# Two node stages of a graph network kernel: work on whole groups of four tiles, or tile by tile

## The chip, the core and the metric

The kernel runs on one core of a Trainium2 chip. The metric is the device time of one execution in microseconds, the median of several runs. The profile is of one execution, taken by the hardware profiler.

## The reference, cut to what matters

Four graph layers follow each other. In each, a node stage makes dense products from normalized node features, and an edge stage gathers and sums over 50000 edges. The node features are `x`, 50000 rows of 256 float32.

```python
def _layernorm(x, axis=-1, eps=1e-05):
    m = jnp.mean(x, axis=axis, keepdims=True)
    v = jnp.var(x, axis=axis, keepdims=True)
    return (x - m) / jnp.sqrt(v + eps)
...
h = jnp.maximum(_layernorm(x), 0.0)
x = x + _L0_gnn_ref(h, ...)
h = jnp.maximum(_layernorm(x), 0.0)
x = x + _L1_gnn_ref(h, ...)      # ends: agg + h @ w_own + bias
h = jnp.maximum(_layernorm(x), 0.0)
x = x + _L2_gnn_ref(h, ...)      # needs h @ W_s.T, h @ W_t.T; ends: agg @ W_fc.T + b_fc
h = jnp.maximum(_layernorm(x), 0.0)
x = x + _L3_gnn_ref(h, ...)      # needs h @ W_forward.T, h @ W_reverse.T
```

The bias of the second layer (`own_bias`) is added to its output only when the third node stage reads it, and the third layer's `b_fc` is added there too, ahead of its time, to the copy of x that the third edge stage will add to (`both_bias` is the sum of the two).

## The kernel before

`node_pass(layer)` is the node stage, called four times with `layer` 0 to 3. The third and the fourth node stage are layers 2 and 3. The rows are cut into tiles of 128 rows (one to a partition) by 256 columns. Four tiles (`G` = 4) make a group, and there are 98 groups. Every buffer with the suffix of a side exists four times (`S` = 4): group c uses side c mod 4, so a side is free again when its use by group c-4 is over.

Each engine runs its own program over the groups through `pipeline`, which takes pairs of a lag and a function. At step c it calls each function on group c minus its lag, in the order of the list. With `by_tile` it calls them all for tile 0, then all for tile 1, and so on. Most steps stand in a hardware loop of four steps, one for each side. Engines meet in semaphores that count up: `then_inc` when an instruction is done, `wait_ge` ahead of the next one.

In layers 2 and 3 the work of a group is this:

- SP loads `x` of the group (L1667). In layer 2 it waits for `bias_in` of the group four before, in layer 3 for `normed` of it. At the end it stores the results: in layer 2 `from_src` and `to_dst` (the two products, L1703), `own` (the tile `biased`, L1699) and `turned` (the rectified and transposed tiles `kept_t`, L1705), 512 KB each; in layer 3 only `h`, 272 KB (L1703). A store waits for `out_made`, ACT's copies of all four tiles. In SP's list, the load of group c comes before the store of group c-6. Every store counts up `t_put` of its side when it has landed.
- DVE, step c, list `[(norm_lag, normalize), (0, average)]` with `norm_lag` = 2: first `normalize` of group c-2, four instructions `tensor_scalar` for `xn` (L1784), the last of which counts up `normed`. Then `average` of group c. In layer 2 `average` begins with `join`: it waits for `x`, for `normed` and for `t_put` of group c-4, and then adds `own_bias` to the whole group for `xc` (L1759) and `both_bias` for `biased` (L1760), each one instruction over 128 x 1024 elements. Then come four `bn_stats` (L1770), four `bn_aggr` (L1774) and one addition for `var` (L1777). Layer 3 has no `join` work: its statistics read `x` itself.
- POOL takes `var` to the power -0.5 (L1890). In layer 2 it also copies keys and issues four indirect stores a group (L1903).
- PE, `work` of group q: for each tile g it first turns the next tile (two transposes of `xn`, L1955; behind tile 3 that is tile 0 of the next group), then does the products of tile g (four matmuls, L1977). `turn` waits for `normed`, the whole group, in layers 2 and 3.
- ACT rectifies each turned tile (L2016) and copies the products of each tile to `out` (L2032 in layer 2, L2035 in layer 3).

In layers 0 and 1 DVE already works by tile, with `normalize_tile` and `average_tile`, and PE is told of each normalized tile by `normed_tile`. In layer 0 DVE's order for each tile is normalizing (L1848), bias on the product (L1861), statistics (L1790).

Of the kernel before, what the change touches and what calls it, by code (L numbers as in the profile page):

```python
# [5 lines left out]
ALU = mybir.AluOpType  # L6
# [6 lines left out]
P = 128  # L13
# [3 lines left out]
D = 256  # L17
# [817 lines left out]
G = 4  # L835
# [59 lines left out]
def pipeline(engine, groups, stages, apart=0, by_tile=False):  # L895

    deepest = max(lag for lag, _ in stages)  # L900
    looped = (groups - apart) // S
    peel = min(looped, -(-(deepest + S) // S))

    def step(i, c):
        live = []
        for lag, stage in stages:
            side = (c - lag) % S
            uses = i + (c - lag - side) // S
            H = uses * S + side
            if isinstance(H, int) and not 0 <= H < groups:  # L910
                continue
            live.append((stage, Group(H, side, uses, groups)))
        for g in range(G if by_tile else 1):
            for stage, q in live:
                stage(q, g) if by_tile else stage(q)

    for s in range(S * peel):
        step(s // S, s % S)
    if looped > peel:
        with engine.Fori(peel, looped) as i:  # L920
            for c in range(S):
                step(i, c)
    for s in range(S * looped, groups + deepest):
        step(s // S, s % S)
# [663 lines left out]
def node_pass(nc, k, layer, x_in, mixed_in=None, tables=()):  # L1588
# [5 lines left out]
    groups = k.NT // G  # L1594
    n_put = len(tables)
# [6 lines left out]
    x = both("x", [P, G, D])  # L1602
    if layer == 1:
        xc, mixed = both("xc", [P, G, D]), both("mixed", [P, G, D])
        small = [[ph.sb(f"small{h}_{n}", [P, G]) for n in range(12)] for h in range(S)]
# [7 lines left out]
    xn = both("xn", [P, G, D])  # L1613
# [36 lines left out]
    with nc.Block() as block:  # L1650
# [63 lines left out]
        def _(dve):  # L1714
# [30 lines left out]
                steps(nc.vector.scalar_tensor_tensor(s[11][:], s[2][:], 1.0, s[7][:], ALU.add, ALU.mult))  # L1745
                steps.end()

            def across(bias):

                return bias[:].rearrange("p (o f) -> p o f", o=1).to_broadcast([P, G, D])  # L1750

            def join(q):

                dve.wait_ge(x_got[q.h], 16 * (q.i + 1))
                if layer == 2:
                    if not q.new:
                        dve.wait_ge(normed, q.last)
                        dve.wait_ge(t_put[q.h], 16 * n_put * q.i)
                    nc.vector.tensor_tensor(xc[q.h][:], x[q.h][:], across(k.own_bias), ALU.add).then_inc(joined, 1)  # L1759
                    nc.vector.tensor_tensor(biased[q.h][:], x[q.h][:], across(k.both_bias), ALU.add).then_inc(bias_in, 1)  # L1760
                    dve.wait_ge(joined, q.H + 1)

            def average(q):

                join(q)
                if not q.new:
                    dve.wait_ge(normed, q.last)
                steps = Steps(dve, averaging, q.H, 2)
                for g in range(G):
                    ins = nc.vector.bn_stats(stats[q.h][:, g, :], source[q.h][:, g, :])  # L1770
                steps(ins)
                dve.sem_inc(stats_in, 1)
                for g in range(G):
                    ins = nc.vector.bn_aggr(moments[q.h][:, g, :], stats[q.h][:, g, :])  # L1774
                steps(ins)
                steps.end()
                nc.vector.tensor_scalar(var[q.h][:], moments[q.h][:, :, 1], 1e-5, None, ALU.add).then_inc(var_made, 1)  # L1777

            def normalize(q):
                dve.wait_ge(std_made, q.H + 1)  # L1780
                if not q.new:
                    dve.wait_ge(turned, G * q.last)
                for g in range(G):
                    ins = nc.vector.tensor_scalar(xn[q.h][:, g, :], source[q.h][:, g, :], moments[q.h][:, g, 0:1],  # L1784
                                                  inv_std[q.h][:, g:g + 1], ALU.subtract, ALU.mult)
                ins.then_inc(normed, 1)

            def tile_stats(q, g):

                return nc.vector.bn_stats(stats[q.h][:, g, :], source[q.h][:, g, :])  # L1790
# [1 line left out]
            def average_tile(q, g):  # L1792

                if g == 0:
                    dve.wait_ge(x_got[q.h], 16 * (q.i + 1) + (16 if layer == 1 and q.final and x_in.shape[0] % P else 0))
                    if not q.new:
                        dve.wait_ge(normed, q.last)
                        if layer == 1:
                            dve.wait_ge(raw_made, G * q.last)
                    if layer == 1:  # L1800
                        ball(q)
                if layer == 1:
                    ins = nc.vector.scalar_tensor_tensor(xc[q.h][:, g, :], mixed[q.h][:, g, :], small[q.h][11][:, g:g + 1],
                                                         x[q.h][:, g, :], ALU.mult, ALU.add)
                    if g < G - 1:
                        ins.then_inc(join_tile, 1)
                    else:
                        ins.then_inc(joined, 1)
                    if g:
                        dve.wait_ge(join_tile, (G - 1) * q.H + g)  # L1810
                        dve.sem_inc(mean_in, 1)
                        tile_stats(q, g - 1)
                    if g < G - 1:
                        return
                    dve.wait_ge(joined, q.H + 1)
                    dve.sem_inc(mean_in, 1)
                ins = tile_stats(q, g)
                if g < G - 1:
                    return
                steps = Steps(dve, averaging, q.H, 2)  # L1820
                steps(ins)
                dve.sem_inc(stats_in, 1)
                for n in range(G):
                    ins = nc.vector.bn_aggr(moments[q.h][:, n, :], stats[q.h][:, n, :])
                steps(ins)
                steps.end()
                nc.vector.tensor_scalar(var[q.h][:], moments[q.h][:, :, 1], 1e-5, None, ALU.add).then_inc(var_made, 1)  # L1827
# [46 lines left out]
            if layer == 1:  # L1874
                pipeline(dve, groups, [(2, clamp_tile), (norm_lag, normalize_tile), (after_lag, own_tile),
                                       (join_lag, average_tile)], by_tile=True)
            elif layer == 0:
                pipeline(dve, groups, [(norm_lag, normalize_tile), (after_lag, bias_tile), (0, average_tile),
                                       (after_lag + 2, pair_tile)], by_tile=True)
            else:  # L1880
                pipeline(dve, groups, [(norm_lag, normalize), (0, average)])

        @block.gpsimd
        def _(pool):
# [58 lines left out]
        @block.tensor  # L1943
        def _(pe):
            def turn(q, g):

                t = G * q.H + g
                if layer <= 1 and g < G - 1:
                    pe.wait_ge(normed_tile, (G - 1) * q.H + g + 1)
                else:  # L1950
                    pe.wait_ge(normed, q.H + 1)
                if not (q.first and g < 2):
                    pe.wait_ge(rectified, t - 1)
                for c in range(2):
                    ins = nc.tensor.transpose(p_turn[g % 2][:, c * P:(c + 1) * P], xn[q.h][:, g, c * P:(c + 1) * P],  # L1955
                                              k.ident[:])
                ins.then_inc(turned, 1)

            def work(q):

                if q.first:
                    turn(q, 0)
                for g in range(G):
                    t = G * q.H + g
                    if g + 1 < G:
                        turn(q, g + 1)
                    elif not q.final:
                        turn(q.next(), 0)
                    pe.wait_ge(rectified, t + 1)
                    if not (q.first and g < banks):  # L1970
                        if layer <= 1:
                            pe.wait_ge(raw_made, t - banks + 1)
                        if layer >= 1:
                            pe.wait_ge(out_made, t - banks + 1)
                    for w, (n, matrix) in enumerate(k.products[layer]):
                        for c in range(2):
                            ins = nc.tensor.matmul(p_out[w][g % banks][:, 0:n], turned_rows(q.h, g)[:, c * P:(c + 1) * P], matrix[:, c, :],  # L1977
                                                   start=c == 0, stop=c == 1)
                    ins.then_inc(product, 1)
            pipeline(pe, groups, [(work_lag, work)], apart=2)  # L1980
# [785 lines left out]
```

## Time and profile before

| | |
|---|---|
| median of 3 runs | 8104.73 us |
| the runs | 8104.73, 8105.07, 8094.45 us |
| profiled execution | 8095.47 us |
| its span | 8093.8 us |
| instructions | 150708 |
| PE busy | 5806.9 us (72%) |
| DVE busy | 5259.3 us (65%) |
| ACT busy | 3347.9 us (41%) |
| POOL busy | 4865.0 us (60%) |
| third node stage in the span | about 3840 to 4665 us |
| fourth node stage in the span | about 6649 to 7005 us |

The shares are means over stages with different limits; what a stage is bound by is read from its own stretch. All times in the rows are microseconds from the start of the span unless a column says ns. PE is matrix work, PEld its loading of weights, DVE the vector engine, ACT the scalar engine, POOL the general engine, SP the engine that issues most transfers (its queue is SPq).

### The profile page before, as it was taken

The numbers are of one execution on the slowest core, as the hardware profiler recorded it, in microseconds if no ns is written. First come the engines' busy times: TensorE is split into PE (matmuls) and PEld (weight loads), VectorE is DVE, ScalarE is ACT, GpSimd is POOL, SyncE is SP. The second block draws the span as 40 slices with busy tenths as digits, with TensorE's granted clock in tenths as the row PEclk, the third lists the DMA queues.
The fourth block names the chain that finished last, engine by engine and source line by source line (L and its number), as shares of the span: only waits on it lengthen the run. The fifth ranks groups of instructions, "written<-read, shape, count | busy, mean of one in ns | idle before, by whom it ended". The sixth has DMA issues, their size and how long they took to land. (4 is left out here: it accounts for less than half of the span.)

```text
span 8093.8 us, 150708 instructions
## 1 busy us (share of the span) xinstructions
PE 5806.9 (72%) x21870; PEld 3548.2 (44%) x21871; DVE 5259.3 (65%) x17471; ACT 3347.9 (41%) x10587; POOL 4865.0 (60%) x6155
## 2 busy tenths in 40 slices
PE   4997899326769999677899967777666779500477
PEld 3773344115544444455444434444224558500365
DVE  4999888324559998355666657666773559633755
ACT  1992255203555554255344433333112567400166
POOL 1556777747652222775777767777467753477443
PEclk7996799668899999899999988988897999855799
DMA  1662000026877776687888866666106878522167
GB/s 60 211 211 57 1 1 1 1 65 220 287 248 243 249 246 231 210 291 272 293 316 317 310 203 202 204 203 204 38 16 215 297 270 229 155 55 55 51 225 238
DMA packets 803185, 1457.11 MB, mean 180 GB/s; under 512 B 137216, under 2 KB 543597, under 8 KB 803030
## 3 DMA queue, kind: packets, MB, share of 16 engines
q1 hardware_dynamic: 462070, 752.88, 28.2%
q10 hardware_dynamic: 188000, 410.91, 14.7%
q0 software_dynamic: 152960, 291.84, 12.9%
q14 instruction: 129, 1.06, 0.0%
q8 instruction: 26, 0.43, 0.0%
HBM read 809.53 MB, written 645.70 MB: 180 GB/s over the span
## 5 line engine op out<-in xcount | busy, mean ns | idle before, releaser
L1280 PE MATMUL merge_banks<-merge_rows,merge_mask 128*128 x6264 | 1607.3, 413 | 648.1 <-SPq L1249 436.0
L1280 PEld LDWEIGHTS merge_banks<-merge_rows,merge_mask 128*128 128x128 f32 x6264 | 1243.5, 205 | 1011.9 <-issue 831.3
L1421 POOL DMA_INDIRECT merge_rows<-h,merge_take_i x1224 | 1173.7, 959 | 472.6 <-issue 316.8
L1262 DVE TENSOR_SCALAR merge_mask<-ramp,dst_at,soft_at_step 128x128 f32<-128x128 f32 x2349 | 851.8, 369 | 912.4 <-PE merge_banks L1280 778.5
L1977 PE MATMUL node_p_out<-w,node_h_t 128*128 128x259 f32 (+2 forms) x4704 | 1433.9, 427 | 14.3 <-ACT node_h_t L2016 12.9
L1344 ACT COPY merge_total<-merge_banks 128x256 f32<-128x256 f32 x1568 | 577.2, 369 | 1076.3 <-PE merge_banks L1280 931.8
L1890 POOL TENSOR_TENSOR node_inv_std<-node_var,node_minus_half 128x4 f32<-128x4 f32 x392 | 453.6, 1157 | 863.1 <-DVE node_var L1827 570.6
L1977 PEld LDWEIGHTS node_p_out<-w,node_h_t 128*128 128x128 f32 x4704 | 745.0, 190 | 267.4 <-issue 212.5
L1955 PE MATMUL node_p_turn<-ident,node_xn 128*128 128x128 f32 x3136 | 619.6, 279 | 189.1 <-DVE node_xn L1784 91.2
L1977 PE MATMUL node_p_out<-w,node_kept_t 128*128 128x512 f32 x1568 | 741.0, 595 | 0.0
L1955 PEld LDWEIGHTS node_p_turn<-ident,node_xn 128*128 128x128 f32 x3136 | 404.1, 141 | 737.7 <-issue 450.7
L1331 ACT COPY merge_banks<-merge_held 128x256 f32<-128x256 f32 x1568 | 587.9, 376 | 258.6 <-issue 134.4
L2207 PE MATMUL score_table<-score_at_high,score_at_low 128*128 128x392 f32 x784 | 387.2, 578 | 287.3 <-DVE score_at_high L2163 278.6
L1903 POOL DMA_INDIRECT src_sorted<-node_key,node_key_at x392 | 420.3, 1072 | 180.1 <-issue 92.7
L2016 ACT ACTIVATE node_h_t<-node_p_turn 128x256 f32<-128x256 f32 x1176 | 448.9, 382 | 142.8 <-PE node_p_turn L1955 137.5
L587 POOL DMA_INDIRECT rank_src_of_src<-ends,rank_src_take_src x392 | 373.7, 953 | 130.8 <-issue 122.8
L593 POOL DMA_INDIRECT rank_src_of_dst<-ends,rank_src_take_dst x392 | 377.2, 962 | 112.0 <-issue 104.7
L2143 POOL DMA_INDIRECT score_b<-to_dst,score_take_b x392 | 372.0, 949 | 119.4 <-issue 119.4
L2141 POOL DMA_INDIRECT score_a<-from_src,score_take_a x392 | 378.8, 966 | 105.0 <-issue 90.3
L2215 PE MATMUL score_p_h<-w,score_h_t 128*128 128x256 f32 x1568 | 440.7, 407 | 0.0
L2326 POOL DMA_INDIRECT score_a<-h,score_take_a x392 | 374.4, 955 | 106.1 <-issue 62.0
L1260 DVE TENSOR_SCALAR merge_mask<-ramp,dst_at 128x128 f32<-128x128 f32 x783 | 292.5, 397 | 201.2 <-PE merge_banks L1280 145.8
(541 smaller groups left out, 10536.2 us busy)
## 6 DMA issues: line engine op xcount, KB each, us to landing
merge_held<-own ACTq DMA_DIRECT2D x196, 512.0 KB, 5.4
x<-merge_total ACTq DMA_DIRECT2D x196, 512.0 KB
node_x<-x SPq DMA_DIRECT2D x196, 512.0 KB, 6.0
node_x<-in_x SPq DMA_DIRECT2D x194, 512.0 KB
h<-node_rows_h SPq DMA_DIRECT2D x98, 512.0 KB, 4.2
merge_held<-h ACTq DMA_DIRECT2D x98, 512.0 KB
mix<-merge_total ACTq DMA_DIRECT2D x98, 512.0 KB
node_mixed<-mix SPq DMA_DIRECT2D x98, 512.0 KB, 3.6
```

The source lines that it names most:

```text
L1262: ins = nc.vector.tensor_scalar(mask[j][:], k.ramp[:, 0:P], columns(k.dst_at, s), columns(weight, s), ALU.is_equal, ALU.mult)
L1280: nc.tensor.matmul(banks[:, bass.ds(nc.s_assert_within(at[2 * j + 1], 0, (BANKS - 1) * 512, skip_runtime_bounds_check_because=small), D)], ...
L1331: nc.scalar.copy(bank(q, g), held[q.held][:, g, :]).then_inc(seeded, 1)
L1344: nc.scalar.copy(total[q.total][:, g, :], bank(q, g)).then_inc(kept, 1)
L1421: nc.gpsimd.indirect_dma_start(rows[:, (j + n) * D:(j + n + 1) * D], None, table, bass.IndirectOffsetOnAxis(take_i[:, j + n:j + n + 1], 0) ...
L1890: nc.gpsimd.tensor_tensor(inv_std[q.h][:], var[q.h][:], minus_half[:], ALU.pow).then_inc(std_made, 1)
L1903: nc.gpsimd.indirect_dma_start(k.src_sorted, bass.IndirectOffsetOnAxis(key_at[:, g:g + 1], 0), key[:, g:g + 1], None, bounds_check=k.NP - ...
L1955: ins = nc.tensor.transpose(p_turn[g % 2][:, c * P:(c + 1) * P], xn[q.h][:, g, c * P:(c + 1) * P], k.ident[:])
L1977: ins = nc.tensor.matmul(p_out[w][g % banks][:, 0:n], turned_rows(q.h, g)[:, c * P:(c + 1) * P], matrix[:, c, :], start=c == 0, stop=c == 1)
L2016: nc.scalar.activation(turned_rows(q.h, g), p_turn[g % 2][:, 0:D], ACT.Relu).then_inc(rectified, 1)
L2207: nc.tensor.matmul(p_table[:, 0:NT], at_low[j % HOT][:], at_high[j % HOT][:], start=first and j == 0, stop=False, skip_group_check=True).t ...
L2215: ins = nc.tensor.matmul(p_h[j % 2][:, 0:D], h_t[side][:, g, c * P:(c + 1) * P], k.w2[:, c, 2 * D:3 * D], start=c == 0, stop=c == 1)
```

## The change

Layers 2 and 3 now use the functions by tile. `join`, `average` and `normalize` (and `across`, which spreads a bias over four tiles) go away. `average_tile` gets layer 2's part: for each tile one addition of `own_bias` for `xc` and one of `both_bias` for `biased`, then the statistics of the tile before. `bias_in` is counted up with the fourth tile's addition. The waits for `normed` and `t_put` of the group four before stand ahead of tile 0's additions. In the list of DVE, `normalize_tile` of group c-2 and `average_tile` of group c are called in turn for each tile. PE's `turn` waits for `normed_tile` for tiles 0 to 2 and for `normed` for tile 3, in all layers.

```diff
-            def across(bias):
-                return bias[:].rearrange("p (o f) -> p o f", o=1).to_broadcast([P, G, D])
-            def join(q):
-                dve.wait_ge(x_got[q.h], 16 * (q.i + 1))
-                if layer == 2:
-                    if not q.new:
-                        dve.wait_ge(normed, q.last)
-                        dve.wait_ge(t_put[q.h], 16 * n_put * q.i)
-                    nc.vector.tensor_tensor(xc[q.h][:], x[q.h][:], across(k.own_bias), ALU.add).then_inc(joined, 1)
-                    nc.vector.tensor_tensor(biased[q.h][:], x[q.h][:], across(k.both_bias), ALU.add).then_inc(bias_in, 1)
-                    dve.wait_ge(joined, q.H + 1)
-            def average(q):
...
-            def normalize(q):
...
@@ average_tile
                         dve.wait_ge(normed, q.last)
                         if layer == 1:
                             dve.wait_ge(raw_made, G * q.last)
+                        elif layer == 2:
+                            dve.wait_ge(t_put[q.h], 16 * n_put * q.i)
                     if layer == 1:
                         ball(q)
-                if layer == 1:
-                    ins = nc.vector.scalar_tensor_tensor(xc[q.h][:, g, :], mixed[q.h][:, g, :], small[q.h][11][:, g:g + 1],
-                                                         x[q.h][:, g, :], ALU.mult, ALU.add)
+                if layer in (1, 2):
+                    if layer == 1:
+                        ins = nc.vector.scalar_tensor_tensor(xc[q.h][:, g, :], mixed[q.h][:, g, :], small[q.h][11][:, g:g + 1],
+                                                             x[q.h][:, g, :], ALU.mult, ALU.add)
+                    else:
+                        ins = nc.vector.tensor_tensor(xc[q.h][:, g, :], x[q.h][:, g, :], k.own_bias[:], ALU.add)
                     if g < G - 1:
                         ins.then_inc(join_tile, 1)
                     else:
                         ins.then_inc(joined, 1)
+                    if layer == 2:
+                        ins = nc.vector.tensor_tensor(biased[q.h][:, g, :], x[q.h][:, g, :], k.both_bias[:], ALU.add)
+                        if g == G - 1:
+                            ins.then_inc(bias_in, 1)
                     if g:
                         dve.wait_ge(join_tile, (G - 1) * q.H + g)
                         dve.sem_inc(mean_in, 1)
@@ the list of DVE
             else:
-                pipeline(dve, groups, [(norm_lag, normalize), (0, average)])
+                pipeline(dve, groups, [(norm_lag, normalize_tile), (0, average_tile)], by_tile=True)
@@ PE
             def turn(q, g):
                 t = G * q.H + g
-                if layer <= 1 and g < G - 1:
+                if g < G - 1:
                     pe.wait_ge(normed_tile, (G - 1) * q.H + g + 1)
                 else:
                     pe.wait_ge(normed, q.H + 1)
```

## Rows read from the trace of the kernel before

**Rows 1.** Two stretches: PE, PEld, DVE, ACT, POOL busy; clock, DMA share, GB/s.

```profile
3900.00:4600.00 700.00, 665.41 (x2018) 309.78 (x2017) 474.66 (x1260) 297.74 (x672) 531.48 (x595) 1.00 0.89 315
...
6680.00:6980.00 300.00, 283.01 (x2044) 243.13 (x2043) 274.42 (x1109) 216.58 (x681) 102.39 (x85) 1.00 0.82 228
```

**Rows 2.** Groups of instructions by line, 3900 to 4600: busy, mean ns, idle before and releaser.

```profile
L1955 PE MATMUL node_p_turn<-ident,node_xn 128*128 128x128 f32 x672 | 131.3, 277 | 34.6 <-DVE node_xn L1784 34.4
...
L1890 POOL TENSOR_TENSOR node_inv_std<-node_var,node_minus_half 128x4 f32<-128x4 f32 x85 | 107.1, 1260 | 11.8 <-DVE node_var L1777 10.8
L1759 DVE TENSOR_TENSOR node_xc<-node_x,own_bias 128x1024 f32<-128x1024 f32 x84 | 103.5, 1232 | 200.3 <-DMA turned<-node_kept_t 200.3
```

**Rows 3.** Timeline of DVE, third stage: start, us, instruction, idle before it and releaser.

```profile
3909.63 1.23 DVE L1759 TENSOR_TENSOR node_xc<-node_x,own_bias 128x1024 f32<-128x1024 f32 x1 [2.09 <-DMA turned<-node_kept_t]
...
4101.67 1.23 DVE L1759 TENSOR_TENSOR node_xc<-node_x,own_bias 128x1024 f32<-128x1024 f32 x1 [2.58 <-DMA turned<-node_kept_t]
...
4103.95 1.40 DVE L1770 BATCH_NORM_STATS2 node_stats<-node_xc 128x6 f32<-128x256 f32 x4
...
4106.52 1.38 DVE L1784 TENSOR_SCALAR node_xn<-node_xc,node_moments,node_inv_std 128x256 f32<-128x256 f32 x4 [0.41 <-issue]
4109.27 1.23 DVE L1759 TENSOR_TENSOR node_xc<-node_x,own_bias 128x1024 f32<-128x1024 f32 x1 [1.37 <-DMA turned<-node_kept_t]
...
4113.71 1.43 DVE L1784 TENSOR_SCALAR node_xn<-node_xc,node_moments,node_inv_std 128x256 f32<-128x256 f32 x4
4118.65 1.23 DVE L1759 TENSOR_TENSOR node_xc<-node_x,own_bias 128x1024 f32<-128x1024 f32 x1 [3.52 <-DMA turned<-node_kept_t]
...
4633.21 1.23 DVE L1759 TENSOR_TENSOR node_xc<-node_x,own_bias 128x1024 f32<-128x1024 f32 x1 [2.02 <-DMA turned<-node_kept_t]
```

**Rows 4.** Timeline of SP's issues, third stage.

```profile
3901.93 0.38 SPq L1703 DMA_DIRECT2D from_src<-node_out  x1
...
4111.07 0.38 SPq L1703 DMA_DIRECT2D from_src<-node_out  x1
...
4626.26 0.38 SPq L1703 DMA_DIRECT2D from_src<-node_out  x1
```

**Rows 5.** Timelines of PE and ACT, third stage.

```profile
4108.03 0.43 PE L1955 MATMUL node_p_turn<-ident,node_xn 128*128 128x128 f32 x2 [0.82 <-DVE node_xn L1784]
...
4110.05 0.38 PE L1955 MATMUL node_p_turn<-ident,node_xn 128*128 128x128 f32 x2
...
4110.25 0.58 ACT L2032 COPY node_out<-node_p_out 128x512 f32<-128x512 f32 x1 [1.36 <-PE node_p_out L1977]
...
4112.18 0.58 ACT L2032 COPY node_out<-node_p_out 128x512 f32<-128x512 f32 x1 [1.07 <-PE node_p_out L1977]
```

**Rows 6.** Timeline of DVE, fourth stage.

```profile
6656.59 1.41 DVE L1770 BATCH_NORM_STATS2 node_stats<-node_x 128x6 f32<-128x256 f32 x4 [3.50 <-DMA node_x<-x]
...
6800.74 1.38 DVE L1784 TENSOR_SCALAR node_xn<-node_x,node_moments,node_inv_std 128x256 f32<-128x256 f32 x4
...
6802.03 1.40 DVE L1770 BATCH_NORM_STATS2 node_stats<-node_x 128x6 f32<-128x256 f32 x4
...
6804.10 1.38 DVE L1784 TENSOR_SCALAR node_xn<-node_x,node_moments,node_inv_std 128x256 f32<-128x256 f32 x4
```

**Rows 7.** Timelines of PE and SP, fourth stage.

```profile
6802.25 0.43 PE L1955 MATMUL node_p_turn<-ident,node_xn 128*128 128x128 f32 x2
6802.30 0.34 SPq L1667 DMA_DIRECT2D node_x<-x  x1
```

**Rows 8.** Timeline of DVE, first node stage.

```profile
404.41 0.42 DVE L1861 TENSOR_TENSOR node_out<-node_p_out,bias 128x259 f32<-128x259 f32 x1
404.75 0.41 DVE L1790 BATCH_NORM_STATS2 node_stats<-node_x 128x6 f32<-128x256 f32 x1
405.08 0.39 DVE L1848 TENSOR_SCALAR node_xn<-node_x,node_moments,node_inv_std 128x256 f32<-128x256 f32 x1
```

**Rows 9.** Transfers issued 6680 to 6980: KB each, median us from issue to landing.

```profile
h<-node_out SPq DMA_DIRECT2D x85, 272.0 KB, 4.3
```

More of the change, by code:

```diff
@@ L1746, in ball @@
                 steps.end()
-            def across(bias):
-                return bias[:].rearrange("p (o f) -> p o f", o=1).to_broadcast([P, G, D])
-            def join(q):
-                dve.wait_ge(x_got[q.h], 16 * (q.i + 1))
-                if layer == 2:
-                    if not q.new:
-                        dve.wait_ge(normed, q.last)
-                        dve.wait_ge(t_put[q.h], 16 * n_put * q.i)
-                    nc.vector.tensor_tensor(xc[q.h][:], x[q.h][:], across(k.own_bias), ALU.add).then_inc(joined, 1)
-                    nc.vector.tensor_tensor(biased[q.h][:], x[q.h][:], across(k.both_bias), ALU.add).then_inc(bias_in, 1)
-                    dve.wait_ge(joined, q.H + 1)
-            def average(q):
[L1765 to L1777, printed above, removed]
-            def normalize(q):
[L1780 to L1786, printed above, removed]
             def tile_stats(q, g):
```

## The prediction

> **What bounds the kernel now.** The change touches only two of the kernel's stages, the node passes of the third and the fourth layer, so I read first the table by stage [rows 1]. Third stage (steady part, 700 us): PE busy 665, DVE 475, DMA share 0.89. Fourth (300 us): PE busy 283, DVE 274. PE looks like the bound in both, but the question in each is who makes it wait.
>
> Third stage, groups of instructions with the idle time before them [rows 2]. 84 groups of four tiles in 700 us: 8.33 us a group. PE waits 34.4 us for `xn`, which is DVE's normalizing; DVE itself waits 200.3 us, 2.4 us a group, before `xc`, and what ends that is the DMA of `turned`, the last of the four stores of the group that used the same side four groups earlier. POOL waits for DVE's variance only 10.8 us in 700. So DVE isn't short of time; it stands behind a landing. The timeline shows the circle. DVE starts `xc` at 4101.67 and ends the normalizing at 4107.90 [rows 3]; PE starts the turn at 4108.03, and the next turn at 4110.05; ACT's copy starts at 4110.25 and takes 0.58; SP issues the store of that group at 4111.07 [rows 4, 5]; it has landed when DVE starts `xc` again, 4118.65 [rows 3]. Sum of the steps: 6.23 + 0.13 + 2.22 (turn, four products, up to ACT's copy) + 0.58 + 0.24 + 7.58 = 16.98 us, for **two** groups. It is two because of places: DVE's `xc` of group c needs the store of c-4; behind it in program order stands the normalizing of c-1, whose tile 0 PE turns before the last tile of c-2, and that tile completes the store on which `xc` of c+2 waits. In the step of 4101.67 DVE came round its loop (4106.52 is 0.4 late); without that the `xc`-to-normalized time is 5.87 (4109.27 to 4113.71 + 1.43). Landing, from the first store's issue to `xc`, is 7.41 us in the mean of 88 pairs; 7.70 in the first of them (3901.93 to 3909.63), 6.95 in the last (4626.26 to 4633.21), 7.58 in the one above [rows 3, 4]. With 7.41 the circle is 16.45 without the turn of the loop and 16.81 with it; half of the mean of both is 8.31, against the 8.33 measured. So the circle through the landing is the bound, not PE, whose own pace is 1.94 a tile (ACT's copies 4110.25 and 4112.18 [rows 5]), 7.74 a group.
>
> Fourth stage. DVE's instructions stand back to back: normalizing 6800.74, statistics 6802.03, next normalizing 6804.10 [rows 6], 3.36 us a group, with some 0.15 between statistics and their aggregate and a gap at the turn of the loop, once in four groups. PE starts its first turn 0.13 after the fourth normalized tile ends (6802.25 against 6802.12) [rows 6, 7]. PE follows DVE there, and DVE waits for nobody: `turned` of four groups back is long there, and 274 us busy with those short gaps fill the 300. DVE's own instructions are the bound.
>
> **The change part by part.** *Fourth stage, order.* Four normalizings, four statistics, four aggregates, one variance: none added or removed. Alone they follow each other every 0.32 (1.38 for four) and 0.33 [rows 6]; interleaved, in the first stage, product-plus-bias, statistics and normalizing start 0.34 and 0.33 after each other [rows 8]. So DVE's 3.36 stays. PE is told of the first tile 1.0 us earlier, but four tiles still come every 3.36, and PE's four take 3.33 (283 us for 85 groups). Gain: only at the very end, the last group, about 1 us. The increments per tile cost nothing beside [rows 8], where they are already made. *What comes later:* `normed` is now told after seven instructions instead of four, at 2.38 instead of 1.38, and the load of `x` waits for it (SP issues at 6802.30 what was told at 6802.12 [rows 7]); the first statistics of the step come at 0.33 instead of 1.30. The load has 2 x 3.36 - 2.38 - 0.18 + 0.33 = 4.5 us instead of 6.5. How long such a load takes isn't shown inside the stage, since nobody waits for it. Bounds: 3.5 on free engines (the first load of the stage [rows 6]), and 4.3 plus some for one that meets a store (the median of the store of `h` [rows 9]). I take 3.5 to 4.3, hidden, cost 0, because the store goes out behind the load, and the one before it went 2.7 us earlier. At 5.0 it would cost (5.0 - 4.5)/2 x 96 = 24 us.
>
> *Third stage, size.* `xc` and `biased` for 1024 elements start every 1.14 ((4103.95 - 4101.67)/2) [rows 3]; an addition of one tile takes 0.34 [rows 8], eight of them 2.7 instead of 2.28: 0.4 us more on DVE in each group. The wait for the tile before is always over (one tile behind), so I set it at nothing; at 0.05 each it would be 0.2 a group, on the old circle only. In the old circle PE no longer waits for the fourth normalized tile but for tile 0, three normalizings less (0.97); but three normalizings of the group before now lie in the body ahead of it (0.97 more). Both cancel, the 0.4 stays, and the old circle would become 17.0 in the mean. That alone is slower than 16.63.
>
> *Third stage, order.* This is the main term. Before, all four tiles of group c-2 were normalized ahead of the wait for the landing of c-4. Now only tile 0 is; tiles 1 to 3 come behind that wait. Queued behind it on DVE: `xc` and `biased` of tile 0, then normalizing 1, done 2 x 0.335 + 0.40 = 1.07 after the landing; tile 2 comes 1.33 later, tile 3 again 1.33, faster than PE's 1.94. Who waits for it: PE's turn of tile 1, and behind that in its queue the product of tile 0 and everything after. New circle: 1.07 + 0.13 + four tiles of PE from the turn of tile 1 up to ACT's last copy (2.02 to the next turn, as 4108.03 to 4110.05, twice 1.94, then 2.13 to the copy, as 4110.05 to 4112.18 [rows 5]: 8.03) + 0.58 + 0.24 + 7.41 = **17.46 us** for the two groups from c-4 to c-2. Nothing of it depends on the loop's turn. Half is 8.73, above the other circle's 8.5; both parities of groups stand under it, while before only one at a time was late. Against 8.33: +0.40 in each of the 94 groups with a landing wait, +38 us. What hides a part: nothing, PE would now wait 1.0 a group.
>
> What could shift the 7.41: with a longer group the same 2.5 MB meet fewer others; the load of `x` waits for `biased` of all four tiles, told 4.5 after the landing instead of 2.3, and goes right behind the four stores as before. Ends from the rows: 6.95, (17.00/2 - 8.33) x 94 = +16 us; 7.70, (17.75/2 - 8.33) x 94 = +51 us. I take the mean of the 88.
>
> The Trainium skill (Perfetto Trace Analysis, Optimizing Scalar/DVE Operations) gives about 60 ns of access overhead for each DVE instruction on SBUF; six more would be an estimated 0.36 us a group where the rows give 0.40, and the sum stays.
>
> **The rivals.** *Faster:* DVE isn't saturated, and PE's 34.4 us of waiting in 700 go, because tile 0 is ahead of the landing wait and told early. That would be 40 us over the 815 us of the stage if PE's 7.74 became the pace, but POOL has only 10.8 us of waiting in 700 [rows 2], which leaves 13; I put it at 8075. It decides if the landing falls under 16.66 - 10.05 = 6.61 us, below each of the three shown. The page just named says that where DVE isn't saturated but makes bubbles on others, breaking up instructions may let work end sooner. Its condition holds here (DVE 475 of 700), its effect needs the broken-up work to lie ahead of the wait, and three of four tiles don't. 10%. *Same:* the landing shrinks to 6.9 or less as stores spread evenly, or PE's wait and the landing overlap better than in the circle: +0 to +16, 14%, about 8108. *Slower still:* as forecast, and the fourth stage's load comes late: DVE waits before its statistics; decides from a load of 4.5 us on, at 5.0 +24 on top, about 8160. The overlap of load and store speaks for it, the DMA share of 0.82 [rows 1] against. 14%.
>
> **How the numbers follow.** The profiled execution takes 8095.5 (span 8093.8). +38 in the third stage, -1 at the end: 8133 (8132.5). The runs' median is 8104.7, two of three near 8105 and one at 8094.5, so I set 4 on top of the profiled time's sum: **8137**. Forecast 62%. The range: from +16 on the profiled execution, less 4 for the lowest run, 8108, to +51 with the higher runs and a part of the last rival, 8168. A difference within 0.2%, 16 us, is about what measurement of this kernel can't tell from none. Faster 0.10, same 0.14, slower 0.76.
>
> **What would show it.** Third stage: 8.6 to 8.9 us a group; PE waits of about 1 us before a turn in nearly every group (before: about every second group), and the turn that waits is the second of a group, not the first; DVE idle before `xc` still ended by `turned`; `xc` a tile op of 0.4 us. Fourth stage: DVE step 3.36 still, PE's wait for `xn` spread thinner, no wait for `x`. Wrong: if landings are under 6.9 us, or if DVE waits for `x` in the fourth stage, or if the third stage's group takes under 8.3.

## The result and the profile after

The changed kernel takes 8175.95 us in the median (8165.82 to 8192.45), the kernel before 8099.59 us in the median of the runs beside it. The ratio is 1.0097, with a 95% interval from 1.0084 to 1.011: slower, by 76 us where 32 were forecast (8137 against 8104.7), and outside the range (8108 to 8168). The profiled execution took 8173.59 us, its span is 8171.9 us, 78 more than before.

The third node stage, from the first clearing of `x` to the first clearing of the stage behind it, took 844.4 us before (3840.07 to 4684.44) and takes 928.7 us now (3828.51 to 4757.21): +84.3. The fourth, up to POOL's first copy behind it, went from 360.3 to 362.3 us. So all of it is in the third.

The steady part of the third stage, as a stretch of 600 us. Columns as in [rows 1]: busy us (instructions) of PE, PEld, DVE, ACT, POOL, then TensorE's granted clock, DMA share, GB/s.

```profile
3950.00:4550.00 600.00, 533.89 (x1558) 247.50 (x1556) 385.50 (x1353) 230.40 (x521) 365.47 (x455) 0.97 0.81 284
```

Every engine does less in a given time than in [rows 1], and the granted clock is 0.97 where it was 1.00. Groups of instructions of the same stretch, with the idle time before them:

```profile
L1859 POOL TENSOR_TENSOR node_inv_std<-node_var,node_minus_half 128x4 f32<-128x4 f32 x65 | 71.5, 1099 | 115.2 <-DVE node_var L1796 114.9
...
L1924 PE MATMUL node_p_turn<-ident,node_xn 128*128 128x128 f32 x518 | 103.5, 282 | 64.8 <-DVE node_xn L1817 64.7
...
L1769 DVE TENSOR_TENSOR node_xc<-node_x,own_bias 128x256 f32<-128x256 f32 x257 | 108.1, 421 | 195.0 <-DMA turned<-node_kept_t 195.0
```

They answer to [rows 2]: PE waits for `xn` 65 us in 600 where it waited 34 in 700, POOL waits 115 us where it hardly waited, and DVE still stands behind the landing of `turned`. A group takes 9.29 us on the average of 85 in the steady part, against 8.32 (9.18 and 8.29 over all 98).

Two rounds of the circle in the timelines of SP, DVE and PE. SP's first store of a group, and its load of `x`:

```profile
4097.29 0.38 SPq L1703 DMA_DIRECT2D from_src<-node_out  x1
...
4105.03 0.38 SPq L1703 DMA_DIRECT2D from_src<-node_out  x1
...
4109.33 0.35 SPq L1667 DMA_DIRECT2D node_x<-x  x1
4114.86 0.38 SPq L1703 DMA_DIRECT2D from_src<-node_out  x1
...
4118.06 1.05 SPq L1667 DMA_DIRECT2D node_x<-x  x1
4122.61 0.38 SPq L1703 DMA_DIRECT2D from_src<-node_out  x1
...
4134.46 0.38 SPq L1703 DMA_DIRECT2D from_src<-node_out  x1
```

DVE, the additions of tile 0 behind the landing, and the normalizing behind them:

```profile
4104.75 0.43 DVE L1769 TENSOR_TENSOR node_xc<-node_x,own_bias 128x256 f32<-128x256 f32 x1 [4.61 <-DMA turned<-node_kept_t]
...
4105.42 0.41 DVE L1817 TENSOR_SCALAR node_xn<-node_xc,node_moments,node_inv_std 128x256 f32<-128x256 f32 x1
...
4112.48 0.42 DVE L1769 TENSOR_TENSOR node_xc<-node_x,own_bias 128x256 f32<-128x256 f32 x1 [1.59 <-DMA turned<-node_kept_t]
...
4118.73 0.41 DVE L1817 TENSOR_SCALAR node_xn<-node_xc,node_moments,node_inv_std 128x256 f32<-128x256 f32 x1 [0.46 <-issue]
4122.63 0.43 DVE L1769 TENSOR_TENSOR node_xc<-node_x,own_bias 128x256 f32<-128x256 f32 x1 [3.50 <-DMA turned<-node_kept_t]
...
4123.31 0.41 DVE L1817 TENSOR_SCALAR node_xn<-node_xc,node_moments,node_inv_std 128x256 f32<-128x256 f32 x1
```

PE, the turns around the two waits:

```profile
4105.96 0.43 PE L1924 MATMUL node_p_turn<-ident,node_xn 128*128 128x128 f32 x2 [1.79 <-DVE node_xn L1817]
...
4108.02 0.38 PE L1924 MATMUL node_p_turn<-ident,node_xn 128*128 128x128 f32 x2
...
4117.71 0.38 PE L1924 MATMUL node_p_turn<-ident,node_xn 128*128 128x128 f32 x2
...
4119.65 0.38 PE L1924 MATMUL node_p_turn<-ident,node_xn 128*128 128x128 f32 x2
...
4123.85 0.43 PE L1924 MATMUL node_p_turn<-ident,node_xn 128*128 128x128 f32 x2 [2.10 <-DVE node_xn L1817]
4124.12 3.39 PE L1946 MATMUL node_p_out<-w,node_kept_t 128*128 128x512 f32 x4
4127.30 0.63 PE L1924 MATMUL node_p_turn<-ident,node_xn 128*128 128x128 f32 x2
```

The first round is the forecast circle, step by step: store 4097.29, landed 4104.75 (7.46), tile 1 normalized 4105.83 (1.08), turn 4105.96 (0.13), next store of that parity 4114.86 (8.90): 17.57 us for two groups, against 17.46 written. The turn that waits is the one of tile 1: the landing wait of DVE stands between the normalizing at 4118.73 (tile 0) and the one at 4123.31 (tile 1). But the wait isn't 1 us in each group. It is whole in every second one, 1.6 to 2.5 us, and the groups between take PE's 7.74. In the second round the products behind the wait take 3.39 us instead of 1.88. The granted clock of that piece and of the one behind it (columns as above):

```profile
4124.00:4127.40 3.40, 3.40 (x7) 1.34 (x7) 3.40 (x12) 0.39 (x1) 1.22 (x2) 0.58 1.08 399
4128.00:4138.00 10.00, 10.00 (x32) 4.74 (x32) 6.76 (x27) 4.41 (x12) 7.25 (x10) 1.00 0.52 183
```

In this trace no wait of 1.85 us and less had one; of the 25 waits from 1.89 to 2.54 us, 17 had one and 8 had none, so the length of the wait alone doesn't decide it.

### The profile page after: what moved, and what is told of

The parts are those of the page before. It is cut to its first block and busy times, and to the rows that moved or that the text cites. A ratio compares the mean times of both kernels' runs of the same rounds, so it can differ in the third digit from the quotient of the medians.

```text
span 8171.9 us, 152298 instructions
## 1 busy us (share of the span) xinstructions
PE 5823.1 (71%) x21870; PEld 3553.9 (43%) x21871; DVE 5295.2 (65%) x18059; ACT 3350.8 (41%) x10587; POOL 4788.4 (59%) x6155
## 3 DMA queue, kind: packets, MB, share of 16 engines
q14 instruction: 130, 1.06, 0.0%
## 5 line engine op out<-in xcount | busy, mean ns | idle before, releaser
L1859 POOL TENSOR_TENSOR node_inv_std<-node_var,node_minus_half 128x4 f32<-128x4 f32 x392 | 426.2, 1087 | 1028.9 <-DVE node_var L1796 1028.4
L1946 PE MATMUL node_p_out<-w,node_kept_t 128*128 128x512 f32 x1568 | 770.7, 615 | 0.0
```

The lines of the kernel that those rows point to most:

```text
L1859: nc.gpsimd.tensor_tensor(inv_std[q.h][:], var[q.h][:], minus_half[:], ALU.pow).then_inc(std_made, 1)
```

## The experiments

Theory A, formed on this trace: the order is the cause. Three of four normalizings stand behind the landing wait, which makes the circle of 17.5 us for two groups; and PE's wait, gathered in every second group, is long enough for its clock to fall. Theory B: the size is the cause, eight small additions in place of two wide ones. Stage lengths below are of the profiled executions, from clearing to clearing as above.

| kernel | us a group, third stage | stage, us | ratio to before (95%) |
|---|---|---|---|
| before | 8.32 | 844.4 | 1 |
| changed | 9.29 | 928.7 | 1.0097 (1.0084 to 1.011) |
| third stage only | 9.16 | 922.0 | 1.0098 (1.0081 to 1.0115) |
| fourth stage only | | | 0.9998 (0.9988 to 1.0007) |
| changed, wide additions | 10.39 | 1034.9 | 1.0225 (1.0208 to 1.0243) |
| changed, two matmuls added | 9.47 | 956.1 | 1.0133 (1.0116 to 1.015) |
| changed, one matmul added | 8.92 | 901.6 | 1.0071 (1.0054 to 1.0088) |
| before, one matmul added | 8.61 | 872.4 | 1.0038 (1.0023 to 1.0052) |
| normalizings first, small additions | 8.16 | 826.2 | 0.9972 (0.9961 to 0.9984) |
| before, PE told of each tile | 7.91 | 808.5 | 0.9939 (0.9923 to 0.9956) |
| changed, late wait | 7.75 | 787.9 | 0.9910 (0.9891 to 0.9929) |
| before, told, late wait | 7.92 | 812.8 | 0.9947 (0.993 to 0.9963) |
| the same, small additions | 7.75 | 791.1 | 0.9922 (0.9906 to 0.9939) |

**Where it is.** The first kernel has the change in the third stage alone, the second in the fourth alone; the functions by group stay beside those by tile. The first is shown here against the changed kernel:

```diff
-                pipeline(dve, groups, [(norm_lag, normalize_tile), (0, average_tile)], by_tile=True)
+                if layer == 2:
+                    pipeline(dve, groups, [(norm_lag, normalize_tile), (0, average_tile)], by_tile=True)
+                else:
+                    pipeline(dve, groups, [(norm_lag, normalize), (0, average)])
...
-                if g < G - 1:
+                if layer <= 2 and g < G - 1:
                     pe.wait_ge(normed_tile, (G - 1) * q.H + g + 1)
```

> Only the third node stage works tile by tile; the fourth is as before. If all of the loss is in the third stage (both theories of its cause): 76 to 84 us over the kernel before, third stage some 928 us long instead of 844. If half of it is elsewhere: 40 us or less.

> Only the fourth node stage works tile by tile. It is bound by DVE's own instructions, whose number does not change, so 0 to +4 us against the kernel before (the traces give 360.3 and 362.3 us for this stage). If the later told load of x mattered as the third rival had it, +20 or more.

8189.9 us (85 over the kernel before beside it, where 76 to 84 were expected) and 8104.3 us, ratios 1.0098 and 0.9998: all of the loss is in the third stage, and the fourth gives neither gain nor loss. Its later load of `x` doesn't matter. The first of the two has the third stage of the changed kernel, and serves as a second sample of the clock: it has 14 falls where the changed kernel has 18, and its stage is 6.7 us shorter, four times 1.7. Its shortest wait with a fall is 1.84 us.

**Size against order.** In the changed kernel, the two additions are wide again, at tile 0; the order stays.

```diff
+                    if layer == 2:
+                        if g == 0:
+                            nc.vector.tensor_tensor(xc[q.h][:], x[q.h][:], across(k.own_bias), ALU.add).then_inc(joined, 1)
+                            nc.vector.tensor_tensor(biased[q.h][:], x[q.h][:], across(k.both_bias), ALU.add).then_inc(bias_in, 1)
+                            return
+                        dve.wait_ge(joined, q.H + 1)
+                        dve.sem_inc(mean_in, 1)
+                        tile_stats(q, g - 1)
```

> The changed kernel, but in the third stage the two additions are again one instruction each over four tiles, both at tile 0; order and the wait for the landing stay. Theory A (order): tile 1 is normalized 2.28 + 0.40 us after the landing instead of 1.07, so the circle of two groups grows by 1.6 to 19.1 us, the waits of PE get longer and its clock falls in more pairs: 75 us or more over the changed kernel, 8250 or more. Theory B (size: six more instructions on DVE and their waits cost the time): 38 us or more faster than the changed kernel.

8287.09 us, 1.0225: less work on DVE, and 110 us slower than the changed kernel. A pair of groups takes 12.98 + 7.74 = 20.7 us: the 19.1 of the circle, and one fall of the clock in every pair. Its stretch, and a turn of PE with the products behind it:

```profile
3950.00:4550.00 600.00, 504.14 (x1389) 233.84 (x1388) 325.97 (x870) 204.42 (x463) 332.36 (x406) 0.91 0.70 253
```

```profile
4100.92 0.53 PE L1933 MATMUL node_p_turn<-ident,node_xn 128*128 128x128 f32 x2 [3.02 <-DVE node_xn L1826]
4101.24 3.56 PE L1955 MATMUL node_p_out<-w,node_kept_t 128*128 128x512 f32 x4
```

Waits are 2.9 us and more here, and all 42 pairs have their fall. A pair without the fall would have taken 15.48 for the work of two groups, 0.3 for the restart and 3.3 of waiting in the mean, 19.1. Theory B is out as the main cause; the small additions even shorten what stands between the landing and tile 1.

**The clock.** Matmuls of which nobody reads the result are put ahead of PE's turn of tile 1, where its wait is. First two a group, then one, then one in the kernel before.

```diff
                 t = G * q.H + g
+                if layer == 2 and g == 1:
+                    for n in range(2):
+                        nc.tensor.matmul(p_fill[:], k.ident[:], k.w2[:, 0, 0:2 * D], start=True, stop=True)
```

> The changed kernel, with two matmuls of 512 columns added ahead of each turn of tile 1 in the third stage (0.94 us of PE work a group; their result is read by nobody). Theory A (the circle of 17.5 us for two groups, plus TensorE's granted clock falling after a wait of 2 us or more, which costs some 1 us a pair): the added work falls into the wait, waits become about 0.1 to 1.2 us in each group instead of 1.6 to 2.5 in every second one, the granted clock stays at 1.00, a pair takes 17.5 to 17.6 instead of 18.6, and the kernel is 40 to 50 us faster than the changed one (about 8125 to 8135) although it does more. Theory B (the slow matmuls come from contention, or more work on DVE is the cause): no gain, between 0 and +88 us on the changed kernel (0.94 x 94).

8215.05 us, 1.0133, slower; 9.46 us in every group, no wait of PE at all. The size of the addition was wrong: two matmuls are four PE instructions and take 1.72 us, not 0.94. With 7.74 + 1.72 = 9.46 PE itself was the bound, above half the circle. Its clock is 1.00, but with PE never idle and PE the bound, the run doesn't say what the falls cost. So the next two add half as much.

> The changed kernel, with one added matmul a group ahead of the turn of tile 1 in the third stage (result read by nobody). The trace of the run with two shows four PE instructions of 1.72 us together, so one is 0.86, and PE's own pace becomes 7.74 + 0.86 = 8.60 us, just under half the circle (8.75). Theory A (the circle, plus a granted clock that falls after waits of about 2 us): waits of 0.1 to 0.3 us in nearly every group, granted clock 1.00, 8.75 to 8.85 us a group instead of 9.29; 40 to 50 us faster than the changed kernel with 98 matmuls more. Theory B (contention or something else makes matmuls slow): no faster than the changed kernel, 9.3 us a group or more.

> The same added matmul in the kernel before, whose granted clock is 1.00 in the third stage already. PE's pace of 8.60 us is above the 8.32 us a group of the circle through the landing, so 8.60 a group: +26 us on the kernel before. If an added matmul helped for another reason than the clock, it would help here too.

In the changed kernel one added matmul a group gives 8162.29 us, 1.0071 against 1.0097 without; the stage is 27 us shorter with 98 matmuls more. In the kernel before it costs: 8141.36 us, 1.0038, the stage 28 us longer, 8.61 us a group as forecast. The stretch of the changed kernel with one:

```profile
3950.00:4550.00 600.00, 591.58 (x1755) 274.22 (x1754) 404.43 (x1420) 242.00 (x540) 374.49 (x471) 1.00 0.85 294
```

The clock is 1.00, the longest wait of PE is 1.24 us, and no products take twice their time. So the falls belong to the gathered waits and are not a matter of transfers (the DMA share is 0.85 here, 0.81 in the changed kernel). The gain is 27 us, not 40 to 50: a group takes 8.92 us, about 0.1 above the forecast, since the landing is 7.70 us in the mean here, not 7.5, and the 9.29 it was set against is the steady part (over all 98 groups it is 9.18 against 8.90).

**Order and telling, one by one.** Both kernels normalize all four tiles ahead of the landing wait and tell PE of each. One has small additions (the changed kernel with `normalize_tile` and `average_tile` called for whole groups), the other wide ones (the kernel before). The edit of the second:

```diff
+                def normalize_group(q):
+                    for g in range(G):
+                        normalize_tile(q, g)
+
-                pipeline(dve, groups, [(norm_lag, normalize), (0, average)])
+                pipeline(dve, groups, [(norm_lag, normalize_group), (0, average)])
...
-                if layer <= 1 and g < G - 1:
+                if g < G - 1:
                     pe.wait_ge(normed_tile, (G - 1) * q.H + g + 1)
```

> The changed kernel, but in both stages DVE normalizes all four tiles first, and only then comes the wait for the landing with the additions by tile. PE is still told of each tile. Theory A: the circle goes back through the next group's normalizing; 5.87 + 0.4 - 0.97 (PE waits for tile 0 only) in place of 5.87, so 15.9 to 16.3 us for two groups against 16.45 to 16.81 before, that is 8.0 to 8.2 us a group: 10 to 30 us faster than the kernel before, granted clock 1.00. Theory B (size): slower than the kernel before by 20 to 40 us.

> The kernel before, with one thing of the change: PE is told of each normalized tile. Theory A: the circle shortens by 0.97 us to 15.5 to 15.8 us, 7.8 to 7.9 us a group, if POOL keeps up; 20 to 45 us faster than before. If POOL is the next bound (it waited for DVE only 10.8 us in 700), 8.2 us a group and 10 to 15 us faster.

8082.69 us (0.9972) and 8057.77 us (0.9939): 21 and 46 us faster than before, theory A's side in both, the second by a little more than its 20 to 45. Theory B wanted the first slower. Telling alone: 8.32 to 7.91 us a group. Small additions on top: 7.91 to 8.16, +0.25, what they cost where the old circle binds; the landing, too, is longer there, 7.63 us in the mean against 7.49, and no run separates the two. The order on top of both: 8.16 to 9.29. The turn's idle time behind `xn` in the two, 3950 to 4550:

```profile
L1932 PE MATMUL node_p_turn<-ident,node_xn 128*128 128x128 f32 x588 | 114.4, 276 | 19.9 <-DVE node_xn L1817 19.5
```

```profile
L1959 PE MATMUL node_p_turn<-ident,node_xn 128*128 128x128 f32 x608 | 117.5, 275 | 4.9 <-DVE node_xn L1848 4.2
```

**The wait moved.** Only `biased` needs the landing, since its old content is what the store reads; `xc` doesn't. So the additions for `biased` and the wait go behind the variance, in the changed kernel and then in the one before (told of each tile).

```diff
-                        elif layer == 2:
-                            dve.wait_ge(t_put[q.h], 16 * n_put * q.i)
...
                 nc.vector.tensor_scalar(var[q.h][:], moments[q.h][:, :, 1], 1e-5, None, ALU.add).then_inc(var_made, 1)
+                if layer == 2:
+                    if not q.new:
+                        dve.wait_ge(t_put[q.h], 16 * n_put * q.i)
+                    for n in range(G):
+                        ins = nc.vector.tensor_tensor(biased[q.h][:, n, :], x[q.h][:, n, :], k.both_bias[:], ALU.add)
+                    ins.then_inc(bias_in, 1)
```

> The changed kernel, but in the third stage the additions for biased, and the wait for the landing that only they need, stand behind the variance, at the end of DVE's step. Everything else is by tile, as changed. Theory A: no normalizing stands behind the wait of its own step; the circle through the end of the step is 1.3 + 0.5 + 0.13 + 2.2 + 0.8 + 7.4 = 12.4 us for two groups and binds no more; PE's 7.74 us or POOL bound, 7.75 to 8.2 us a group: 15 to 55 us faster than the kernel before, PE hardly waits. Theory B (size): DVE has the same instructions as in the changed kernel, so no gain on the changed kernel.

> The kernel before, with PE told of each tile, and in the third stage the one wide addition for biased with its wait for the landing moved behind the variance. Theory A: as the one by tile, not bound by the landing: 7.75 to 8.2 us a group, 15 to 55 us faster than before, within 10 us of the one by tile; the smaller number of instructions gives nothing more, since DVE waits anyway. Theory B: clearly faster than the one by tile, by 30 us or more.

By tile: 8033.23 us, 0.9910, the fastest of all, 71 us faster than before where 15 to 55 were forecast; its stage is 56.5 us shorter. 7.75 us a group is PE's own pace, and PE waits for nothing. Order by tile isn't bad in itself; what was bad is the wait in the middle of it. The wide one reaches 8064.01 us, 0.9947, 31 us behind it and not within 10: fewer instructions on DVE, and slower. Theory B, which wanted the wide one ahead, fails again, but theory A had no reason for this either. Against telling alone, the moved wait gave the wide kernel nothing: 7.92 us a group after 7.91. The trace points at POOL. DVE's normalizing in the wide one waits for POOL:

```profile
L1850 DVE TENSOR_SCALAR node_xn<-node_xc,node_moments,node_inv_std 128x256 f32<-128x256 f32 x301 | 104.0, 409 | 159.6 <-POOL node_inv_std L1896 159.6
```

POOL is never idle for DVE there, and its fourth indirect store of a group takes 1.73 us instead of 0.97 (the mean of 73 such in 600 us), each time begun 0.3 to 0.4 us into DVE's wide addition for `biased`:

```profile
4102.29 0.97 POOL L1909 DMA_INDIRECT src_sorted<-node_key,node_key_at  x1 [0.30 <-issue]
4103.56 1.73 POOL L1909 DMA_INDIRECT src_sorted<-node_key,node_key_at  x1 [0.30 <-issue]
4105.30 1.06 POOL L1896 TENSOR_TENSOR node_inv_std<-node_var,node_minus_half 128x4 f32<-128x4 f32 x1
```

```profile
4103.24 1.22 DVE L1779 TENSOR_TENSOR node_biased<-node_x,both_bias 128x1024 f32<-128x1024 f32 x1
```

So the last kernel cuts both additions into four, and nothing else:

```diff
-                    nc.vector.tensor_tensor(xc[q.h][:], x[q.h][:], across(k.own_bias), ALU.add).then_inc(joined, 1)
+                    for g in range(G):
+                        ins = nc.vector.tensor_tensor(xc[q.h][:, g, :], x[q.h][:, g, :], k.own_bias[:], ALU.add)
+                    ins.then_inc(joined, 1)
...
-                    nc.vector.tensor_tensor(biased[q.h][:], x[q.h][:], across(k.both_bias), ALU.add).then_inc(bias_in, 1)
+                    for g in range(G):
+                        ins = nc.vector.tensor_tensor(biased[q.h][:, g, :], x[q.h][:, g, :], k.both_bias[:], ALU.add)
+                    ins.then_inc(bias_in, 1)
```

> The kernel before with PE told of each tile and the addition for biased moved behind the variance, as measured already (7.92 us a group, DVE waiting for POOL's power), but with both additions cut into four. If the wide additions hold POOL up (its indirect stores of 1.72 us end with them), they take about 1.1 to 1.3 us now, POOL's round gets shorter by 0.2 to 0.4 us and PE's 7.74 is reached: 7.75 to 7.80 us a group, 10 to 18 us faster than with wide ones. If POOL's round has another cause, 7.9 us a group as before, or more by the added instructions.

8047.05 us, 0.9922; 7.75 us a group, and the indirect stores 1.06 us in the mean instead of 1.18. That is 0.5 us less for the four of a group; POOL's power takes 1.29 us instead of 1.06, so POOL's round shrinks by less, from 7.92 to 7.75. The additions for `biased` also fall elsewhere on POOL's round now: they wait for the landing again (116 us in 600), which the wide ones never did. The run doesn't separate their size from their place. As the two kernels stand, small additions are the better ones where POOL's round is the bound, and the worse ones where the old circle is.

## Why the prediction was wrong

- *What bounds the kernel now* held: the circle of two groups through the landing in the third stage, DVE's own instructions in the fourth. Telling PE earlier (0.97 us off the circle, 0.49 a group) gave 0.41 us a group.
- *Fourth stage: no cost, load of `x` hidden* held: ratio 0.9998 with the change in that stage alone. The rival of the late load is out.
- *Third stage, order* held in its mechanism and nearly in its size: 17.57 us in the round shown, against 17.46.
- **The step that failed** is the one behind it: "both parities of groups stand under it", "PE would now wait 1.0 a group". A circle over two groups fixes the sum of two, not each. The kernel before already showed its waits in every second group, and the changed one gathers them likewise: 0 in one group and 1.6 to 2.5 us in the next. The sum of two groups is the same either way, so this wouldn't have cost anything, had a wait of 2 us the price of two waits of 1. It hasn't: TensorE's clock falls behind many of them. The sum had no term for the clock at all. In all 98 groups there are 18 falls of 1.7 us, 31 us; filling the waits took them away and gave 27 us back.
- *The landing of 7.41 us* was too small. For the stores whose landing decides (those ahead of a short group) it is 7.70 us in the mean of 41, for the others 7.28. That adds 0.29 to the circle, 0.14 a group, some 14 us. The stores that take longer are those with the load of `x` sooner behind (issued 3.1 us after the first store, against 4.5). But in the kernel before the load comes 3.1 to 3.3 us behind every first store, and in the changed kernel with wide additions 3.2 to 3.3, and the landings there are 7.42 and 7.34 us in the mean of 94. So the place of the load alone doesn't explain it, and why they take longer is open.
- The three together: 38 forecast, 31 for the clock, 14 for the landing, 83 of the 84.3 us measured in the stage. It is a sum of estimates; only the one for the clock has a run that takes it away.
- *Third stage, size*: 0.4 us more on the old circle of two groups, so 0.2 a group; measured 0.25 a group, a longer landing included, between the kernel told with wide additions and the one with small. What I left out is the other side of it: POOL's round was shorter with small additions in the kernels with the late wait.
- *Rivals.* "Faster" took POOL for the next bound, because it hardly waited for DVE: 13 us to gain, which is 8.2 us a group. That was no bound: with PE told of each tile the group took 7.91.
- The Trainium skill (Perfetto Trace Analysis, Optimizing Scalar/DVE Operations) says that breaking up instructions may help where DVE isn't saturated but makes others wait. With the landing wait moved to the end of the step the runs agree: 0.9922 with the additions broken up, 0.9947 with wide ones. With the wait ahead of the additions they go the other way: 0.9972 with the additions broken up, 0.9939 with wide ones, and 1.0097 with all work interleaved by tile.

## What to carry to other kernels

Before interleaving two steps by tile, look for the slowest wait of one of them: all that is interleaved behind it now waits too, on its engine and on whoever reads it. Put such a wait at the end of the step and ahead of only the instruction that needs it. A circle over two groups sets the sum of two; the whole idle time can gather in one piece, as it did here, so price what a long gap does to TensorE's clock.

## What the runs showed of the hardware that was not expected

- After PE waits of under 1.84 us in the third stage the products behind took 1.88 to 1.97 us. Behind 31 of the 52 waits from 1.84 to 2.54 us in the changed kernel and the one changed in the third stage only, and behind all of 2.9 us and more in the one with wide additions, products took 2.6 to 3.7 us, with a granted clock of 0.58 in the piece read; each fall cost about 1.7 us. This leaves out the start of the stage. An added matmul of 0.86 us a group in the gap made the stage 27 us shorter, and the same one without such gaps made it 28 us longer.
- In the kernel with the wide late addition, an indirect store of POOL takes 0.97 us, and 1.73 where it begins 0.3 us into DVE's addition of 128 x 1024 float32. Not every overlap has this price: 75 stores that DVE's addition for `xc` overlapped by 0.8 us took 1.06 us. With the additions in pieces of 256 elements the mean fell from 1.18 to 1.06 us. The Trainium skill (SBUF — State Buffer, Who interferes with whom) says that a DVE instruction with two inputs in SBUF contends with a GpSimd instruction that reads SBUF, over a port the two share. The trace agrees in 73 stores and not in the 75: the addition has two such inputs, and POOL's instruction grew by 0.76 us beside it. That the port is the cause wasn't tested.
